# Retention heads one after the other, and the layer norms' work dealt out anew between DVE, ACT and POOL

## The chip, the cores and the metric

The kernel runs on the 8 cores of one Trainium2 chip, each core with its own sequence of 2048 tokens and a full copy of the weights; no core talks to another. Each core has TensorE (PE), VectorE (DVE), ScalarE (ACT), GpSimd (POOL) and a queue for transfers (SP). The metric is the device time of one launch in microseconds, that of the slowest core.

## What is computed

Two layers on x of shape (8, 2048, 1024), each an attention part and a feed-forward part with a plain layer norm (no scale or bias) behind each residual sum:

```python
# layer 0, attention part: an inner network of 2 blocks (i = 0, 1)
ln_x = layer_norm(x, ln1_g[i], ln1_b[i])
q, k, v, xo = split(ln_x @ proj_w[i] + proj_b[i], 4)      # 16 heads of 64
scores = einsum('bhld,bhmd->bhlm', q, k) * D               # D[n, m] = gamma_h**(n-m), 0 where m > n
ret = einsum('bhlm,bhmd->bhld', scores, v) * silu(xo)      # no softmax
x = x + ret @ reto_w[i] + reto_b[i]
h = layer_norm(x, ln2_g[i], ln2_b[i])
x = x + gelu(h @ ffn1_w[i] + ffn1_b[i]) @ ffn2_w[i] + ffn2_b[i]
# then layer_norm(x, lnf_g, lnf_b)
# layer 0, feed-forward: top-2 of 8 experts + shared expert
# layer 1: softmax attention over 1024 columns; block-diagonal rails, gelu, w_cproj
# x = _layernorm(x + part(x)) behind each of the four parts
```

## The kernel before

Activations lie feature-major: SX holds x in fp32 as 8 column tiles (ft) of 128 features by 2048 tokens, and the tokens are worked on in NB = 4 blocks (nb) of 512. A1, A2, A3 and PP hold bf16 operands, WR a ring of weights, pb0 to pb5 are PSUM banks of 128 x 512 fp32. The program is one list of instructions per engine, written in the order of the source; each engine runs its own list strictly in order. Every instruction of DVE, ACT and POOL waits for its own engine's previous one and for the tokens given (a token is a semaphore and a count). `bank_done` notes when a buffer is free, `bank_guard` returns that as a wait. `b.block()` makes all engines meet. Weights are issued on POOL's queue, so they stand behind POOL's compute instructions; masks, parking and the output are issued on SP's.

*Layer norm, `emit_ln`,* runs nine times. Five are affine (ln1 and ln2 of both blocks, lnf: scale and bias, result in bf16 in A1), four are plain (result in fp32 in SX, and a bf16 copy in A1). For each nb: eight casts to bf16 (L404 on ACT for ft 0, 3, 6, L407 on DVE for 1, 4, 7 and on POOL for 2, 5), eight squares on ACT (L420, two buffers), sixteen matmuls against a column of 1/1024 for mean and mean square (L425, L414, L431); then a chain on one row: ACT square L437, DVE L443 and L447, ACT logarithm and exponential L450 and L453, two broadcasting matmuls L460 and L464, two ACT copies of -mean and 1/std into SBUF (L469, L472). `emit_apply` adds and multiplies each of the eight tiles with these (L368, L371; even ft on DVE, odd on POOL) and is written one block late: the apply of block nb-1 stands in the source behind the copies of block nb, and the last two follow each other at the end. In affine norms ACT then scales each tile (L379). In plain norms the bf16 copy of a tile (L375) is made by the engine that did *not* apply it, so DVE and POOL wait for each other in each list.

*Retention, in `emit_l0_attn`,* runs for 2 blocks x 8 pairs of heads. Behind the four projections and 16 transposes of v comes, for each of 4 query blocks nb, a loop over key chunks mc = 0 to 4nb+3 of 128 keys. Per chunk and head h there is a score matmul (L954: 64 rows of q and k, head 0 on rows 0 to 63, head 1 on rows 64 to 127, into its own bank), an eviction to bf16 in MB (L973 on ACT for chunks below the diagonal, L980 on DVE with a mask for the four on it) and an accumulation (L933: all 128 rows, 64 columns, head 0 into partitions 0 to 63 of the result bank, head 1 into 64 to 127), two chunks behind its score. Both heads of a chunk are written next to each other; two chunks' slots form the ring. Then ACT copies the result out (L991) and DVE multiplies it with the gate (L996). Over nb that makes 8, 16, 24 and 32 (head, chunk) items.

*Layer-1 attention* begins by parking SX in DRAM (behind all of the norm before it) and by two small matmuls (L582) that spread the bias of v over PF (L587), the buffer in which the norm kept its -mean and 1/std.

## Time and profile before

| | us |
|---|---|
| median of the two runs | 10336.73 |
| lowest, highest run | 10178.47, 10494.99 |
| the profiled execution, its own time | 10140.04 |
| its span on the slowest core (core 4) | 10138.5 |
| spans of the other cores | 10075.2 to 10116.0 |
| stretch 150 to 1312 us, projections and retention of block 0 | 1162.00, PE busy 898.46, clock 0.64 |
| stretch 1312.00 to 1413.20, one affine norm | 101.20, PE 35.48, ACT 65.75, DVE 48.44, POOL 48.22 |
| stretch 4411.70 to 4559.60, one plain norm | 147.90, PE 35.77, ACT 40.64, DVE 41.27, POOL 55.62 |

How to read the rows further on. Times are microseconds from the start of the span. A timeline row gives start, duration (of all the instructions merged in it), engine, source line, operation, output <- input, shapes and count, and in brackets the idle time of the engine before it and what ended it. Matmuls are pipelined: their durations include filling the array, so the distance between starts says more than the duration. The clock is the share of TensorE's full speed that was granted; 0.50 is 1.2 GHz and 1.00 is 2.4 GHz. PEld are weight loads.

### The profile page before, as it was taken

The page shows a single profiled execution, that of the slowest core. Times are in us where ns is not written, and L with a number is a line of the kernel's source. Part 1 is how long each engine was busy: PE and PEld are TensorE (multiplying, and loading weights), DVE is VectorE, ACT ScalarE, POOL GpSimd, SP SyncE. Part 2 cuts the span into 40 slices and gives each one's busy share as a digit, 9 for nine tenths or more (in the row PEclk, how much of TensorE's full clock was granted, in tenths as well). Part 3 has the DMA queues.
Part 4 walks back from the last instruction along what each step waited for, and adds up shares of the span by engine and source line. Part 5 has one row for each costly group of instructions (what it writes and reads, how often), then busy time and mean ns, then how long its engine had stood idle before and what let it go on. Part 6 is the DMA issues. An engine that isn't in the chain of part 4 may idle for free. (4 is left out here: it accounts for less than half of the span.)

```text
span 10138.5 us, 89181 instructions; the slowest of 8 cores (10075.2 to 10138.5 us)
## 1 busy us (share of the span) xinstructions
PE 6911.8 (68%) x25254; PEld 2542.5 (25%) x25254; DVE 2044.2 (20%) x3440; ACT 2270.5 (22%) x3847; POOL 1086.0 (11%) x1144
## 2 busy tenths in 40 slices
PE   3777757767777577625778998874666347777774
PEld 1222212322222122202233443331222112222221
DVE  2222221122222301131111111211111212221222
ACT  3333230023333210232121222121111231112112
POOL 2000020010000200140011122121000210000002
PEclk7666667776666788857889999986777557787876
DMA  2000001101001011101111111201111111111110
GB/s 84 17 17 17 15 13 21 22 12 23 17 17 19 11 23 21 17 34 17 25 27 37 38 26 30 46 9 48 21 25 17 40 24 21 19 21 19 19 19 33
DMA packets 91864, 249.38 MB, mean 25 GB/s; under 512 B 13120, under 2 KB 15840, under 8 KB 87520
## 3 DMA queue, kind: packets, MB, share of 16 engines
q0 software_dynamic: 82688, 190.00, 11.2%
q1 hardware_dynamic: 8720, 53.68, 1.4%
q8 instruction: 239, 3.92, 0.2%
q14 instruction: 217, 1.78, 0.1%
HBM read 407.91 MB, written 25.72 MB: 43 GB/s over the span
## 5 line engine op out<-in xcount | busy, mean ns | idle before, releaser
L549 PE MATMUL pb<-A,WR 128*128 128x512 bf16 x5120 | 1419.2, 435 | 724.5 <-DMA WR<-ffn 207.1
L549 PEld LDWEIGHTS pb<-A,WR 128*128 128x128 bf16 x5120 | 547.0, 108 | 1595.3 <-issue 1245.2
L1570 PE MATMUL pb<-A,PP 128*128 128x512 bf16 x2688 | 669.7, 416 | 204.4 <-DMA PP<-wcT 148.0
L954 PE MATMUL pb<-PP 64*128 64x512 bf16 x1280 | 618.1, 596 | 88.8 <-ACT MB L973 42.9
L1069 PE MATMUL pb<-A,WR 128*128 128x512 bf16 x2048 | 533.0, 429 | 200.9 <-DMA WR<-ffn 200.9
L1578 DVE TENSOR_TENSOR SX<-SX,pb 128x512 f32<-128x512 f32 x512 | 352.2, 688 | 1470.5 <-PE pb L1570 1470.5
L1439 PE MATMUL pb<-A,WR 128*128 128x512 bf16 x2048 | 495.3, 408 | 170.1 <-DMA WR<-fc 170.1
L1530 ACT ACTIVATE A<-pb 128x512 bf16<-128x512 f32 x512 | 305.8, 597 | 1322.5 <-PE pb L1522 1247.6
L933 PE MATMUL pb<-MB,PP 128*64 128x512 bf16 x1280 | 473.3, 628 | 69.1 <-DVE MB L980 69.1
L425 PE MATMUL pb<-A,OM 128*1 128x512 bf16 x288 | 163.7, 588 | 518.3 <-ACT A L404 372.4
L980 DVE TENSOR_TENSOR MB<-pb,PF 128x512 bf16<-128x512 f32 x512 | 354.0, 691 | 710.2 <-PE pb L933 566.7
L973 ACT ACTIVATE MB<-pb 128x512 bf16<-128x512 f32 x768 | 458.6, 597 | 137.2 <-ACT MB L973 66.2
L1358 PE MATMUL pb<-A 128*128 128x512 bf16 x2048 | 455.3, 381 | 4.2 <-DMA A<-fc 4.2
L1380 PE MATMUL pb<-A 128*128 128x512 bf16 x2048 | 452.5, 379 | 0.0
L1035 ACT ACTIVATE A<-pb,CB 128x512 bf16<-128x512 f32 x256 | 175.9, 687 | 1152.0 <-PE pb L549 1122.4
L1570 PEld LDWEIGHTS pb<-A,PP 128*128 128x128 bf16 x2688 | 280.1, 105 | 594.0 <-issue 333.8
L1570 PE MATMUL pb<-A,WR 128*128 128x512 bf16 x1408 | 353.3, 418 | 109.0 <-DMA WR<-wcT 62.7
L1401 POOL TENSOR_TENSOR A<-A,PP 128x512 bf16<-128x512 bf16 x256 | 295.4, 1154 | 841.5 <-DVE A L1398 841.5
L1069 PEld LDWEIGHTS pb<-A,WR 128*128 128x128 bf16 x2048 | 218.2, 108 | 515.6 <-issue 354.4
L1368 ACT ACTIVATE A<-pb 128x512 bf16<-128x512 f32 x256 | 152.9, 597 | 868.1 <-PE pb L1358 866.7
L1522 PE MATMUL pb<-A 128*128 128x512 bf16 x512 | 261.5, 526 | 123.2 <-ACT A L1530 93.2
L1088 DVE TENSOR_TENSOR SX<-SX,pb 128x512 f32<-128x512 f32 x192 | 132.0, 688 | 1014.5 <-PE pb L1069 1014.5
(163 smaller groups left out, 6046.1 us busy)
## 6 DMA issues: line engine op xcount, KB each, us to landing
WR<-ffn POOLq DMA_DIRECT2D x128, 256.0 KB, 4.1
A<-fc POOLq DMA_DIRECT2D x8, 4096.0 KB, 22.5
PP<-wcT POOLq DMA_DIRECT2D x42, 512.0 KB, 5.2
WR<-w POOLq DMA_DIRECT2D x36, 512.0 KB, 5.2
A<-xpark SPq DMA_DIRECT2D x4, 4096.0 KB
WR<-fc POOLq DMA_DIRECT2D x32, 512.0 KB, 5.7
WR<-wcT POOLq DMA_DIRECT2D x22, 512.0 KB, 5.3
SX<-xin SPq DMA_DIRECT2D x1, 8192.0 KB
```

Source lines behind the costliest of these rows:

```text
L549: st=(kt == 0), sp=(kt == Kt - 1): e.matmul(bank[:, 0:512], sl[:, kt * 128:kt * 128 + 128], rhs, start=st, stop=sp),
L933: rbank=rbank: e.matmul(rbank[64 * h:64 * h + 64, 0:512], P1[:, mc * 128 + 64 * h: mc * 128 + 64 * h + 64], sT[2 * (mc % 2) + h], start=(m ...
L954: sb=sb: e.matmul(sb[:, 0:512], P3[64 * h:64 * h + 64, mc * 128:mc * 128 + 128], P2[64 * h:64 * h + 64, nb * 512:nb * 512 + 512], start=Tr ...
L973: e.activation(st, sb[:, 0:512], AF.Copy),
L980: off=off: e.tensor_mul(st, sb[:, 0:512], self.PF[:, off * 512:off * 512 + 512]),
L1069: e.matmul(bank[:, 0:512], sl[:, c * 128:c * 128 + 128], self.A2[:, c * T + nb * 512: c * T + nb * 512 + 512], start=st, stop=sp),
L1358: e.matmul(bank[:, 0:512], self.A3[:, (i * FT + kt) * 128: (i * FT + kt) * 128 + 128], self.A1[:, kt * T + nb * 512: kt * T + nb * 512 + 512],
L1380: e.matmul(bank[:, 0:512], self.A3[:, ((i + 8) * FT + kt) * 128: ((i + 8) * FT + kt) * 128 + 128], self.A1[:, kt * T + nb * 512: kt * T + ...
L1439: e.matmul(bank[:, 0:512], sl[:, it * 128:it * 128 + 128], self.A2[:, it * 2048 + nb * 512: it * 2048 + nb * 512 + 512], start=st, stop=sp ...
L1530: e.activation(self.A2[:, ci * 2048 + nb * 512: ci * 2048 + nb * 512 + 512], bk[:, 0:512], AF.Gelu),
L1570: e.matmul(bank[:, 0:512], sl[:, ci * 128:ci * 128 + 128], self.A2[:, ci * 2048 + nb * 512: ci * 2048 + nb * 512 + 512], start=st, stop=sp ...
L1578: e.tensor_add(self.SX[:, dt * T + nb * 512:dt * T + nb * 512 + 512], self.SX[:, dt * T + nb * 512:dt * T + nb * 512 + 512], bank[:, 0:512 ...
```

## The change

Four edits.

1. `emit_apply`: DVE applies six tiles and POOL two (ft 2 and 6). In plain norms the bf16 copies of tiles 2 and 6 are made by POOL, of 4 and 7 by DVE, of 0, 1, 3 and 5 by ACT. The casts in front of the statistics alternate between ACT (even ft) and DVE (odd); POOL has none.
2. The copies of -mean and 1/std go from ACT (L469, L472) to DVE.
3. The layer-1 attention's bias matmuls also wait for the end of the norm.
4. Retention: the loop runs over single items, all chunks of head 0 and then all of head 1. The ring has four single slots, and an accumulation stands four items behind its score.

```diff
@@ -362,7 +362,7 @@
         def emit_apply(nb, at, mtile, rtile):
             for ft in range(FT):
                 s = slice(ft * T + nb * 512, ft * T + nb * 512 + 512)
-                eng = ("vector", "gpsimd")[ft % 2]
+                eng = "gpsimd" if ft in (2, 6) else "vector"
                 sem = self.esem(eng)
                 tgt = self.SX if kind == "plain" else dst
                 b.emit(eng, lambda e, s=s, tgt=tgt, mtile=mtile: e.tensor_add(
@@ -371,9 +371,16 @@
                 b.emit(eng, lambda e, s=s, tgt=tgt, rtile=rtile: e.tensor_mul(
                     tgt[:, s], tgt[:, s], rtile), inc=((sem, 1),))
                 if kind == "plain":
-                    eng2 = ("gpsimd", "vector")[ft % 2]
-                    b.emit(eng2, lambda e, s=s: e.tensor_copy(
-                        self.A1[:, s], self.SX[:, s]), wait=(sem.tok(),))
+                    if ft in (2, 6):
+                        b.emit("gpsimd", lambda e, s=s: e.tensor_copy(
+                            self.A1[:, s], self.SX[:, s]))
+                    elif ft in (4, 7):
+                        b.emit("vector", lambda e, s=s: e.tensor_copy(
+                            self.A1[:, s], self.SX[:, s]))
+                    else:
+                        b.emit("scalar", lambda e, s=s: e.activation(
+                            self.A1[:, s], self.SX[:, s], AF.Copy),
+                            wait=(sem.tok(),))
                 if kind == "affine":
                     et = sem.tok()
                     b.emit("scalar", lambda e, s=s, ft=ft: e.activation(
@@ -398,7 +405,7 @@
             sqtok = [None] * FT
             for ft in range(FT):
                 s = slice(ft * T + nb * 512, ft * T + nb * 512 + 512)
-                ceng = ("scalar", "vector", "gpsimd")[ft % 3]
+                ceng = ("scalar", "vector")[ft % 2]
                 csem = self.esem(ceng)
                 if ceng == "scalar":
                     b.emit("scalar", lambda e, s=s: e.activation(
@@ -466,13 +473,13 @@
                 wait=rt, inc=((self.s_pe, 1),))
             self.bank_done(None, self.s_pe.tok(), ("SRr", par))
             bt = self.s_pe.tok()
-            b.emit("scalar", lambda e, pmean=pmean, mtile=mtile: e.activation(
-                mtile, pmean[:, 0:512], AF.Copy),
+            b.emit("vector", lambda e, pmean=pmean, mtile=mtile: e.tensor_copy(
+                mtile, pmean[:, 0:512]),
                 wait=(bt,) + self.bank_guard(None, ("PTm", par)))
-            b.emit("scalar", lambda e, psq=psq, rtile=rtile: e.activation(
-                rtile, psq[:, 0:512], AF.Copy),
+            b.emit("vector", lambda e, psq=psq, rtile=rtile: e.tensor_copy(
+                rtile, psq[:, 0:512]),
                 wait=self.bank_guard(None, ("PTr", par)))
-            at = self.s_act.tok()
+            at = self.s_dve.tok()
             self.bank_done(pmean, at)
             self.bank_done(psq, at)
             self.warm(wb, (at,))
@@ -583,7 +590,8 @@
                 bk[:, 0:512], self.O1[:],
                 self.MB[0:1, h * 512:h * 512 + 512],
                 start=True, stop=True),
-                wait=(dt0,) + self.bank_guard(bk), inc=((self.s_pe, 1),))
+                wait=(dt0,) + self.bank_guard(bk)
+                + getattr(self, "ln_done", ()), inc=((self.s_pe, 1),))
             b.emit("scalar", lambda e, h=half, bk=bk: e.activation(
                 self.PF[:, h * 512:h * 512 + 512], bk[:, 0:512], AF.Copy),
                 wait=(self.s_pe.tok(),), inc=((self.s_act, 1),))
@@ -922,70 +930,62 @@ (retention, the inner loops)
                 for nb in range(NB):
                     rbank = self.pb[4 + nb % 2]
-                    M = 4 * nb + 4
...
-                    def emit_mm2(mc, rbank=rbank, nb=nb, M=M):
-                        for h in range(2):
-                            b.emit("tensor", lambda e, h=h, mc=mc,
-                                   rbank=rbank: e.matmul(
-                                rbank[64 * h:64 * h + 64, 0:512],
-                                P1[:, mc * 128 + 64 * h:
-                                   mc * 128 + 64 * h + 64],
-                                sT[2 * (mc % 2) + h],
-                                start=(mc == 0), stop=(mc == M - 1),
-                                skip_group_check=True),
-                                wait=(evtok[mc][h],)
...
-                    for mc in range(M):
-                        for h in range(2):
-                            sb = self.pb[2 * (mc % 2) + h]
...
-                        mmt = self.s_pe.tok()
-                        if mc >= 2:
-                            emit_mm2(mc - 2)
-                        off = mc - 4 * nb
-                        stg = self.bank_guard(None, ("sTp", mc % 2))
-                        for h in range(2):
...
-                    for mc in range(max(0, M - 2), M):
-                        emit_mm2(mc)
+                LK = 4
...
+                    items = [(h, mc) for h in range(2)
+                             for mc in range(4 * nb + 4)]
+                    n_it = len(items)
+                    evtok = [None] * n_it
+
+                    def emit_mm2(i, rbank=rbank, items=items, nb=nb):
+                        h, mc = items[i]
+                        fs = (mc == 0)
+                        b.emit("tensor", lambda e, h=h, mc=mc, fs=fs, i=i:
+                               e.matmul(
+                            rbank[64 * h:64 * h + 64, 0:512],
+                            P1[:, mc * 128 + 64 * h:mc * 128 + 64 * h + 64],
+                            sT[i % LK], start=fs, stop=(mc == 4 * nb + 3)),
+                            wait=(evtok[i],)
...
+                    for i, (h, mc) in enumerate(items):
+                        sb = self.pb[i % LK]
...
+                        b.emit("tensor", lambda e, h=h, mc=mc, nb=nb, sb=sb:
+                               e.matmul(
+                            sb[:, 0:512],
+                            P3[64 * h:64 * h + 64, mc * 128:mc * 128 + 128],
+                            P2[64 * h:64 * h + 64, nb * 512:nb * 512 + 512],
+                            start=True, stop=True),
+                            wait=w0 + self.bank_guard(sb),
+                            inc=((self.s_pe, 1),))
                         mmt = self.s_pe.tok()
+                        if i >= LK:
+                            emit_mm2(i - LK)
+                        st = sT[i % LK]
+                        stg = self.bank_guard(st, ("sTm", i % LK))
...
+                        if off < 0:
+                            b.emit("scalar", lambda e, sb=sb, st=st:
+                                   e.activation(st, sb[:, 0:512], AF.Copy),
+                                   wait=(mmt,) + stg)
...
+                        else:
+                            b.emit("vector", lambda e, sb=sb, st=st, off=off:
+                                   e.tensor_mul(
+                                st, sb[:, 0:512],
+                                self.PF[:, off * 512:off * 512 + 512]),
+                                wait=(mmt, mskf) + stg)
...
+                    for i in range(max(0, n_it - LK), n_it):
+                        emit_mm2(i)
```

## Rows read from the trace of the kernel before

**Rows 1.** The page, part 1: busy us, share of span, instructions of each engine.

```profile
PE 6911.8 (68%) x25254; PEld 2542.5 (25%) x25254; DVE 2044.2 (20%) x3440; ACT 2270.5 (22%) x3847; POOL 1086.0 (11%) x1144
```

**Rows 2.** Window: length, busy PE PEld DVE ACT POOL, granted clock, DMA share, GB/s.

```profile
219.06:293.40 74.34, 64.06 (x160) 13.46 (x160) 23.76 (x36) 31.05 (x52) 1.09 (x3) 0.50 0.05 8
```

**Rows 3.** Timeline, PE, one pair's retention: start, us, engine, line, out<-in, count.

```profile
228.01 1.04 PE L954 MATMUL pb<-PP 64*128 64x512 bf16 x4
...
249.38 0.64 PE L933 MATMUL pb<-MB,PP 128*64 128x512 bf16 x2
249.96 0.60 PE L954 MATMUL pb<-PP 64*128 64x512 bf16 x1
250.42 0.58 PE L954 MATMUL pb<-PP 64*128 64x512 bf16 x1
250.93 0.64 PE L933 MATMUL pb<-MB,PP 128*64 128x512 bf16 x2
```

**Rows 4.** Timeline, ACT and DVE in retention: the two kinds of score eviction.

```profile
220.91 0.69 DVE L980 TENSOR_TENSOR MB<-pb,PF 128x512 bf16<-128x512 f32 x1 [0.24 <-DVE MB L980]
...
250.48 1.34 ACT L973 ACTIVATE MB<-pb 128x512 bf16<-128x512 f32 x2 [0.20 <-ACT MB L973]
...
292.34 0.60 ACT L991 ACTIVATE PT<-pb 128x512 bf16<-128x512 f32 x1 [8.21 <-PE pb L933]
```

**Rows 5.** Timeline, ACT, first affine norm: one whole turn of its loop.

```profile
111.25 0.59 ACT L437 ACTIVATE PF<-pb 1x512 f32<-1x512 f32 x1 [0.84 <-PE pb L431]
...
116.50 0.60 ACT L469 ACTIVATE PF<-pb 128x512 f32<-128x512 f32 x1 [1.64 <-PE pb L464]
...
118.11 7.54 ACT L379 ACTIVATE A<-A,CB 128x512 bf16<-128x512 bf16 x8
...
135.97 0.59 ACT L437 ACTIVATE PF<-pb 1x512 f32<-1x512 f32 x1 [1.05 <-PE pb L431]
```

**Rows 6.** Timeline, DVE, in that turn: alone, then beside POOL.

```profile
116.98 0.69 DVE L368 TENSOR_TENSOR A<-SX,PF 128x512 bf16<-128x512 f32 x1 [0.17 <-DVE A L371]
...
118.64 1.50 DVE L368 TENSOR_TENSOR A<-SX,PF 128x512 bf16<-128x512 f32 x1 [0.17 <-DVE A L371]
...
121.81 4.08 DVE L407 CAST A<-SX 128x512 bf16<-128x512 f32 x3
```

**Rows 7.** Timeline, end of the second affine norm and the stage behind it.

```profile
1394.49 0.60 ACT L469 ACTIVATE PF<-pb 128x512 f32<-128x512 f32 x1 [1.67 <-PE pb L464]
...
1409.46 2.21 POOL L96 DMA_DIRECT2D WR<-ffn  x4 [0.63 <-POOL A L371]
1409.47 3.70 ACT L379 ACTIVATE A<-A,CB 128x512 bf16<-128x512 bf16 x4 [1.46 <-DVE A L371]
...
1418.69 6.57 PE L549 MATMUL pb<-A,WR 128*128 128x512 bf16 x21 [22.40 <-DMA WR<-ffn]
```

**Rows 8.** Timeline, DVE, last plain norm: one turn of its loop and its end.

```profile
10033.55 0.69 DVE L443 TENSOR_TENSOR pb<-pb,PF 1x512 f32<-1x512 f32 x1 [8.40 <-ACT PF L437]
...
10046.28 0.43 DVE L375 CAST A<-SX 128x512 bf16<-128x512 f32 x1 [3.72 <-POOL SX L371]
...
10058.42 1.93 DVE L407 CAST A<-SX 128x512 bf16<-128x512 f32 x3
10068.32 0.69 DVE L443 TENSOR_TENSOR pb<-pb,PF 1x512 f32<-1x512 f32 x1 [7.97 <-ACT PF L437]
...
10116.19 0.43 DVE L375 CAST A<-SX 128x512 bf16<-128x512 f32 x1 [3.72 <-POOL SX L371]
```

**Rows 9.** Timeline, what starts behind two of the plain norms.

```profile
6935.31 0.58 POOL L96 DMA_DIRECT2D MB<-b3row  x1 [0.57 <-POOL SX L371]
6957.73 2.68 POOL L96 DMA_DIRECT2D WR<-w  x5 [21.84 <-ACTq L119]
...
8145.77 0.58 POOL L96 DMA_DIRECT2D PP<-makerT  x1 [0.58 <-POOL SX L371]
...
8154.66 0.33 PE L1480 MATMUL pb<-A,PP 16*16 16x64 bf16 x2 [50.93 <-PEq L119]
```

More of the change, by code:

```diff
@@ L924, in emit_l0_attn @@
                 sT = [self.MB[:, i * 512:(i + 1) * 512] for i in range(4)]
+                LK = 4
                 for nb in range(NB):
                     rbank = self.pb[4 + nb % 2]
-                    M = 4 * nb + 4
-                    evtok = [[None, None] for _ in range(M)]
-                    def emit_mm2(mc, rbank=rbank, nb=nb, M=M):
-                        for h in range(2):
-                            b.emit("tensor", lambda e, h=h, mc=mc,
-                                   rbank=rbank: e.matmul(
-                                rbank[64 * h:64 * h + 64, 0:512],
-                                P1[:, mc * 128 + 64 * h:
-                                   mc * 128 + 64 * h + 64],
-                                sT[2 * (mc % 2) + h],
-                                start=(mc == 0), stop=(mc == M - 1),
-                                skip_group_check=True),
-                                wait=(evtok[mc][h],)
-                                + (self.bank_guard(rbank)
-                                   if mc == 0 else ()),
-                                inc=((self.s_pe, 1),))
-                        self.bank_done(None, self.s_pe.tok(),
-                                       ("sTp", mc % 2))
@@ L947, in emit_l0_attn @@
-                    for mc in range(M):
-                        for h in range(2):
-                            sb = self.pb[2 * (mc % 2) + h]
-                            w0 = ()
-                            if nb == 0 and mc == 0 and h == 0:
-                                w0 = qk_attn + (vtm_done,)
-                            b.emit("tensor", lambda e, h=h, mc=mc, nb=nb,
-                                   sb=sb: e.matmul(
-                                sb[:, 0:512],
-                                P3[64 * h:64 * h + 64,
-                                   mc * 128:mc * 128 + 128],
-                                P2[64 * h:64 * h + 64,
-                                   nb * 512:nb * 512 + 512],
-                                start=True, stop=True),
-                                wait=w0 + self.bank_guard(sb),
-                                inc=((self.s_pe, 1),))
+                    items = [(h, mc) for h in range(2)
+                             for mc in range(4 * nb + 4)]
@@ new lines, in emit_l0_attn @@
+                    n_it = len(items)
[9 more added lines that the diff above has]
+                            wait=(evtok[i],)
+                            + (self.bank_guard(rbank)
+                               if (fs and h == 0) else ()),
+                            inc=((self.s_pe, 1),))
+                        self.bank_done(None, self.s_pe.tok(), ("sTm", i % LK))
@@ new lines, in emit_l0_attn @@
+                    for i, (h, mc) in enumerate(items):
+                        sb = self.pb[i % LK]
+                        w0 = (qk_attn + (vtm_done,)) \
+                            if (nb == 0 and i == 0) else ()
+                        b.emit("tensor", lambda e, h=h, mc=mc, nb=nb, sb=sb:
[5 more added lines that the diff above has]
+                            wait=w0 + self.bank_guard(sb),
+                            inc=((self.s_pe, 1),))
```

22 lines of the change are left out of this document (4 added, 18 removed).

## The prediction

> **What bounds the kernel now.** I read the list of cores first (all eight end close together, so one core can stand for all), then the page, then windows, then the timeline of the stages that the diff touches. TensorE (PE) is busy 68% of the span, ACT 22%, DVE 20% [rows 1], so outside the norms every stage is paced by PE or by the weights it waits for; the diff leaves those stages alone. It touches three places.
>
> *Retention* (16 head pairs, each over 74.3 us) runs with PE busy 64.06 of 74.34 us and the granted clock at 0.50, the lower level of 1.2 GHz, throughout [rows 2]. The reader is to see that "busy" hides a concurrency: four L954 matmuls of about 0.60 each take 1.04 together, so the two heads of a pair (rows 0-63 and 64-127) run side by side, and the next two start 1.04 - 0.60 = 0.44 later. The two L933 matmuls (columns 0-63 and 64-127) take 0.64 together in the same way [rows 3]. A turn of one key chunk, two heads, lasts 250.93 - 249.38 = 1.55 us [rows 3], which is two ACT evictions (1.34 and a gap of 0.20) [rows 4]: the evicting engine is the bound, at 0.77 an item, or 0.69 + 0.24 = 0.93 where DVE masks [rows 4].
>
> *Affine norms* (five) go round an ACT chain: 24.7 us from one L437 to the next, of which eight L379 take 7.54 [rows 5]. *Plain norms* (four) go round a lockstep of DVE and POOL: DVE stands 3.72 us before each L375 cast, waiting for POOL's multiply [rows 8].
>
> **Retention, after.** Heads run one after the other, so no two neighbouring matmuls can run side by side: consecutive L954s share the same 64 rows, L933s the same 64 columns. In the steady part each item is one score matmul and one accumulation, alternating. The trace shows both gaps between starts: L954 to L933, 250.93 - 250.42 = 0.51; L933 to L954, 249.96 - 249.38 = 0.58 [rows 3]. Together 1.09 us per item, more than 0.77 and 0.93: PE becomes the bound. Block nb has n = 8(nb+1) items: four scores to start (4 x 0.44), n - 4 items at 1.09, four accumulations to end (the first 0.14 earlier than an alternation would put it, then 3 x 0.44), and a switch (0.58). That is 1.09n - 0.84 (4 x 0.44 - 4.36 - 0.14 + 1.32 + 0.58 = -0.84). For n = 16, 24, 32 it gives 16.6 + 25.3 + 34.0 = 75.9 us. Before, the same three blocks last from 228.01 [rows 3] to 292.34 [rows 4], 64.3. The first block (n = 8, masked only) stays with DVE at 0.93 an item and costs nothing. So +11.6 per pair, x16 = **+186 us**. The deeper ring (four single slots) gives evictions slack, which no longer matters once PE binds. The bounds: matmuls of one kind with no switching cost would make 0.88 per item, then the evictions bind and the change is about 0; full durations end to end, 0.60 + 0.64 = 1.24 [rows 3], would make 72 items x 0.15 = 10.8 more per pair, +173 on top, +359. I take 1.09, since these very transitions are in the rows. The Trainium skill, page TensorEngine Tiling, section Key Properties, says that a change of tiling mode drains the engine; taken strictly that is the 1.24 of the upper bound, and the sum would be 359 instead of 186.
>
> **Affine norms, after.** A turn is counted from L437. The broadcast copies come at +5.25 (116.50 - 111.25) [rows 5], now on DVE. The trace has no such copy; it lies between DVE's cast of 0.43 [rows 8] and its PSUM operation of 0.69 [rows 4]. I take 0.69, it reads the same fp32 PSUM bank. Two end at +6.8, when ACT's two did. But DVE ran the apply of the block before *ahead* of that point (L368 at 116.98 is its third column tile) [rows 6]; now it stands behind the copies in DVE's queue and has six tiles instead of four. One tile (add and multiply) takes 118.64 - 116.98 = 1.66 us alone and 121.81 - 118.64 = 3.17 beside a working POOL [rows 6]. POOL's two tiles of the new block start at the same moment and take two of DVE's with them: 2 x 3.17 + 4 x 1.66 = 13.0, so DVE ends at +19.9. Behind each tile stands ACT's L379; the last ends one L379 later (7.54 / 8 = 0.94), +20.9, and only then does ACT start the next block's casts and squares. Those took 135.97 - (118.11 + 7.54) = 10.3 [rows 5]; with a fourth ACT cast, partly in its waits for PE, 10.8. Turn: 31.7 against 24.7, +7.0. Two such turns in five norms: **+70**. If POOL did not slow DVE, the turn would be 3.0 shorter: +40.
>
> The end of the norm: before, 1413.17 - 1394.49 = 18.7 us from the last copies to the last L379 [rows 7]. After: 1.7 + 13.0 + 10.0 (six tiles alone) + 1.0 = 25.7. PE, though, did not start at 1413.17 but at 1418.69, 9.2 us after POOL had issued the weights [rows 7]. POOL ends its share by 1394.49 + 1.7 + 2 x 3.2 = 1402.6, so weights are there by 1411.8, and PE starts when the norm ends, 1420.2: +1.5 instead of +7.0. The early DMA gives back most. Four norms that stand before weights: +6; the fifth, before a parked-input transfer that waits for the whole norm: +7. Affine norms in all **+83**.
>
> **Plain norms, after.** No cast crosses between DVE and POOL any more, so the 3.72 us waits go. Turn from one L443: copies at +4.6 (5.25 less 0.69), done at +6.1; six tiles, two contended (13.0), two casts of 0.43 and gaps (1.2), and 0.8 for POOL's casts in the same ports: 15.0, +21.1; then as before 10068.32 - 10058.42 = 9.9 from the next casts [rows 8], and 0.5 for ACT's extra cast: 31.6 against 34.8. Two turns in four norms: -26. The end: before 10116.62 - 10068.32 = 48.3 [rows 8]; after 6.1 + 15.0 + 11.2 = 32.3: -16, x4 = -64. ACT's four casts per block lie beside DVE's tiles. Where POOL issues a load behind the norm, as for the rail weights (issued 8145.77, PE 8154.66), it now issues it while DVE still works: -8 [rows 9]. In all **-98**.
>
> **The added guard** in the layer-1 attention costs nothing: the next weights are issued at 6957.73, after the parking transfer of about 22 us that itself waits for the norm [rows 9]; two small matmuls and two evictions lie under it. Without that cover it would cost them, some 2.5 us.
>
> **Sum.** 186 + 83 - 98 = +171. The profiled execution took 10140.04 us: 10311. The two runs shown have the median 10336.73 (10178.47 and 10494.99), 1.9% above the profiled one; on their scale 10508. I give the middle, **10410**, since the rows can't say which the next runs resemble. Relative to like: +1.7%. About 2% is what a measurement of this kernel can tell from no change.
>
> **The rivals.**
> *Full drain* (slower): item 1.24, retention +359, net +344, +3.4%, 10484 to 10680. For it: each matmul lasts 0.60 or more. Against: starts 0.51 and 0.58 apart. It decides from about 1.12 per item upwards (net +203, 2%). 0.15.
> *Free switch* (no change): single matmuls follow at 0.44 whatever the kind; evictions bind, retention 0, net -15. For it: the measured gaps are always those of pairs. 0.15.
> *Quiet ports* (no change): POOL's fewer operations rarely meet DVE's, turns 3.0 shorter, ends 3.0 shorter: 9 norms x 9 = -80, net about +90. Against: both start on the same copy. 0.12.
> *Higher clock* (faster): with PE issuing without a pause in retention, the clock rises, PE stops binding, and with head runs alternating, ACT's and DVE's evictions overlap. Evictions alone, 0.77 x 8nb + 7.4, are 13.6 + 19.7 + 25.9 = 59.2; about three items overlapped at each of three turns (2.2 us each) save 6.6 per block, and some 1.5 per block is lost at its ends: 44, so -20 per pair, -320, and net -335: -3.3%, 9805 to 10000. Against: 0.50 over a stretch with PE busy 86% [rows 2]. The Trainium skill, TensorE: Matmul & The Clock Gate, Part 1, says that the throttled clock is the default and activity releases it; by that rule this rival would come true. 0.08.
>
> **How the numbers follow.** My forecast has 0.50, with its own range of 10200 to 10590 (net +60 to +250 on the two scales). Slower by over 2%: the full drain and a third of my own, 0.33. Faster by over 2%: the higher clock and a little, 0.09. Within: 0.58. The range drops the higher clock and the upper end of the full drain: free switch on the lower scale is 10125, forecast and half of the drain's reach 10600. I take 10150 to 10600.
>
> **What would show it.** Right: retention's L954 and L933 starts alternate at 0.51 and 0.58, the stretch of one pair about 86 us with PE busy nearly all of it, clock 0.50; affine norm turns near 31.7 with DVE the releaser of L379; plain turns near 31.6, no 3.72 waits. Wrong: a clock above 0.50 in retention; matmuls of different heads overlapping; L379 runs of eight without gaps.

## The result, and the profile after

| | before | after |
|---|---|---|
| median, us | 10419.21 (10 runs, 10091.11 to 10494.99) | 10364.17 (11 runs, 10302.50 to 10665.32) |
| the profiled execution | 10140.04 | 10290.51 |
| span, median of its eight cores | 10096.1 | 10271.8 |
| like with like | 1 | 1.0193, 95% interval 1.0135 to 1.0251 |

In many executions of either kernel the cores of one die or both run at a lower granted clock and take up to 6% longer, so the medians stand the wrong way round, the last row leaves those executions out, and "undisturbed cores" here are the four of a die at the highest clock seen for its kernel. Like with like the changed kernel is 1.9% slower. The interval lies clear of no change, but it contains 2%, so on which side of 2% the change lies stays undecided. Undisturbed cores of the kernel before take 10059 to 10110 us (clock 0.76 to 0.77), those of the changed one 10248 to 10308 (the same clock).

The page of the changed kernel, part 1 and the groups of retention (part 5: line, engine, operation, count, busy us, mean ns, idle time before and what ended it). L945 is the accumulation, L960 the score, L975 and L981 the two evictions:

```profile
PE 7160.2 (70%) x25254; PEld 2603.1 (25%) x25254; DVE 2231.1 (22%) x3660; ACT 2293.2 (22%) x3875; POOL 854.2 (8%) x896
...
L945 PE MATMUL pb<-MB,PP 128*64 128x512 bf16 x1280 | 745.6, 618 | 19.8 <-DVE MB L981 19.7
L960 PE MATMUL pb<-PP 64*128 64x512 bf16 x1280 | 699.1, 580 | 29.1 <-ACT MB L975 12.7
...
L975 ACT ACTIVATE MB<-pb 128x512 bf16<-128x512 f32 x768 | 459.0, 598 | 446.2 <-PE pb L945 387.1
L981 DVE TENSOR_TENSOR MB<-pb,PF 128x512 bf16<-128x512 f32 x512 | 354.2, 692 | 882.4 <-PE pb L945 834.6
```

PE's busy time rose from 6911.8 [rows 1] to 7160.2 for the same number of matmuls, and in retention PE hardly waits any longer, 19.8 and 29.1 us in 1280 matmuls each. The two groups of the kernel before (page, part 5) had 88.8 and 69.1:

```profile
L954 PE MATMUL pb<-PP 64*128 64x512 bf16 x1280 | 618.1, 596 | 88.8 <-ACT MB L973 42.9
...
L933 PE MATMUL pb<-MB,PP 128*64 128x512 bf16 x1280 | 473.3, 628 | 69.1 <-DVE MB L980 69.1
```

Both evicting engines wait for PE instead, 446 and 882 us (137 and 710 before). That is the change of bound that the prediction named. Two pairs' stretches (windows; PE, PEld, DVE, ACT, POOL busy, granted clock), answering to [rows 2]:

```profile
235.42:320.80 85.38, 81.18 (x160) 17.99 (x160) 23.83 (x36) 31.08 (x52) 1.18 (x3) 0.55 0.04 7
799.10:876.26 77.16, 72.26 (x160) 17.40 (x160) 23.84 (x36) 31.08 (x52) 1.18 (x3) 0.65 0.04 8
```

and the steady part (timeline, PE), answering to [rows 3]:

```profile
252.51 0.63 PE L945 MATMUL pb<-MB,PP 128*64 128x512 bf16 x1
253.08 0.60 PE L960 MATMUL pb<-PP 64*128 64x512 bf16 x1
253.62 0.63 PE L945 MATMUL pb<-MB,PP 128*64 128x512 bf16 x1
```

One item takes 253.62 - 252.51 = 1.11 us, 0.57 from accumulation to score and 0.54 on to the next accumulation (over many items 1.10). The 16 stretches of this core sum to 1368.6 us against 1190.5 before, so retention costs **+178**.

One turn of the first affine norm (timeline; L444 and L386 answer to L437 and L379 of [rows 5], the DVE rows to [rows 6], L476 is a copy):

```profile
87.36 0.59 ACT L444 ACTIVATE PF<-pb 1x512 f32<-1x512 f32 x1 [0.83 <-PE pb L438]
97.44 0.81 ACT L386 ACTIVATE A<-A,CB 128x512 bf16<-128x512 bf16 x1 [6.59 <-DVE A L371]
...
120.06 0.59 ACT L444 ACTIVATE PF<-pb 1x512 f32<-1x512 f32 x1 [1.05 <-PE pb L438]
...
92.33 0.69 DVE L476 COPY PF<-pb 128x512 f32<-128x512 f32 x1 [2.81 <-PE pb L471]
...
93.99 1.78 DVE L368 TENSOR_TENSOR A<-SX,PF 128x512 bf16<-128x512 f32 x1 [0.17 <-DVE PF L479]
95.88 1.47 DVE L371 TENSOR_TENSOR A<-A,PF 128x512 bf16<-128x512 bf16 x1
...
106.94 0.69 DVE L371 TENSOR_TENSOR A<-A,PF 128x512 bf16<-128x512 bf16 x1
```

The turn lasts 120.06 - 87.36 = 32.7 us (24.7 before), and ACT, which went round without a pause, now waits for DVE in front of L386. From the start of a norm to the next matmul of other work the five affine norms take 125.8, 127.6, 127.4, 127.8 and 127.2 us, against 111.1, 107.6, 108.2, 106.5 and 102.4: **+100**. The last plain norm (timeline, ACT and DVE), answering to [rows 8]:

```profile
10201.18 0.59 ACT L444 ACTIVATE PF<-pb 1x512 f32<-1x512 f32 x1 [1.05 <-PE pb L438]
...
10233.39 0.59 ACT L444 ACTIVATE PF<-pb 1x512 f32<-1x512 f32 x1 [1.04 <-PE pb L438]
...
10264.36 0.63 ACT L381 ACTIVATE A<-SX 128x512 bf16<-128x512 f32 x1 [3.22 <-DVE SX L371]
...
10266.03 0.43 DVE L378 CAST A<-SX 128x512 bf16<-128x512 f32 x1
```

Its turn is 32.2 us, the whole norm 127.2 instead of 147.9, and the waits of 3.72 are gone. Four norms give back 83, and PE starts 3 us earlier behind the first and 8.5 earlier behind the one ahead of the rail weights: **-95**. The sum, 178 + 100 - 95 = +183, stands beside +176 between the medians of the cores' spans.

### The profile page after: what moved, and what is told of

Read it like the earlier page. It is cut to its first block and busy times, and to the rows that moved or that the text cites. A ratio compares the mean times of both kernels' runs of the same rounds, so it can differ in the third digit from the quotient of the medians.

```text
span 10288.6 us, 89699 instructions; the slowest of 8 cores (10256.0 to 10288.6 us)
## 1 busy us (share of the span) xinstructions
PE 7160.2 (70%) x25254; PEld 2603.1 (25%) x25254; DVE 2231.1 (22%) x3660; ACT 2293.2 (22%) x3875; POOL 854.2 (8%) x896
## 5 line engine op out<-in xcount | busy, mean ns | idle before, releaser
L556 PE MATMUL pb<-A,WR 128*128 128x512 bf16 x5120 | 1384.5, 427 | 742.6 <-DMA WR<-ffn 165.8
L945 PE MATMUL pb<-MB,PP 128*64 128x512 bf16 x1280 | 745.6, 618 | 19.8 <-DVE MB L981 19.7
L960 PE MATMUL pb<-PP 64*128 64x512 bf16 x1280 | 699.1, 580 | 29.1 <-ACT MB L975 12.7
L1069 PE MATMUL pb<-A,WR 128*128 128x512 bf16 x2048 | 516.8, 419 | 201.0 <-DMA WR<-ffn 201.0
L1439 PE MATMUL pb<-A,WR 128*128 128x512 bf16 x2048 | 497.1, 409 | 168.2 <-DMA WR<-fc 168.2
L975 ACT ACTIVATE MB<-pb 128x512 bf16<-128x512 f32 x768 | 459.0, 598 | 446.2 <-PE pb L945 387.1
L981 DVE TENSOR_TENSOR MB<-pb,PF 128x512 bf16<-128x512 f32 x512 | 354.2, 692 | 882.4 <-PE pb L945 834.6
L1570 PE MATMUL pb<-A,WR 128*128 128x512 bf16 x1408 | 352.9, 418 | 107.8 <-DMA WR<-wcT 62.4
```

The source lines that it names most:

```text
L556: st=(kt == 0), sp=(kt == Kt - 1): e.matmul(bank[:, 0:512], sl[:, kt * 128:kt * 128 + 128], rhs, start=st, stop=sp),
L945: e.matmul(rbank[64 * h:64 * h + 64, 0:512], P1[:, mc * 128 + 64 * h:mc * 128 + 64 * h + 64], sT[i % LK], start=fs, stop=(mc == 4 * nb + 3)),
L960: e.matmul(sb[:, 0:512], P3[64 * h:64 * h + 64, mc * 128:mc * 128 + 128], P2[64 * h:64 * h + 64, nb * 512:nb * 512 + 512], start=True, sto ...
L975: e.activation(st, sb[:, 0:512], AF.Copy),
L981: e.tensor_mul(st, sb[:, 0:512], self.PF[:, off * 512:off * 512 + 512]),
L1069: e.matmul(bank[:, 0:512], sl[:, c * 128:c * 128 + 128], self.A2[:, c * T + nb * 512: c * T + nb * 512 + 512], start=st, stop=sp),
```

## The experiments

**The norms alone, and retention alone.** The first kernel has edits 1 to 3 without 4, the second edit 4 alone.

```diff
 # norms alone: the retention loops are those of the kernel before
 # retention alone, against the changed kernel:
...
-                ceng = ("scalar", "vector")[ft % 2]
+                ceng = ("scalar", "vector", "gpsimd")[ft % 3]
...
 # and the other lines of edits 1 to 3 as in the kernel before
```

> The changed kernel with the retention loop of the kernel before. Theory A (the three terms of the prediction add up and do not touch each other): each retention stretch back to 74.3 us from 86, the five affine norms stay near 127 us and the four plain ones near 127, so the profiled time lies about 178 us under that of the changed kernel and within 15 us of the kernel before (+100 for the affine norms with what follows them, -95 for the plain ones); ratio to before 0.998 to 1.003. Rival B (norm changes cost more than their own stretches, through later weights or a lower clock behind them): ratio above 1.006 with the stretches as in theory A.

> The kernel before with the retention loop of the changed kernel. Theory A: 16 stretches of about 86 us instead of 74.3, all norms as before; ratio to before 1.016 to 1.020. Rival B (retention is slowed by something that the norm changes bring, such as the order in which DVE is handed work): stretches below 80 us and a ratio below 1.008.

The norms alone: undisturbed cores 10062 to 10097 us, which is the kernel before. Windows of a retention stretch, of an affine and of a plain norm:

```profile
232.19:306.98 74.79, 64.06 (x160) 13.46 (x160) 23.83 (x36) 31.05 (x52) 1.18 (x3) 0.50 0.05 8
1291.70:1418.40 126.70, 36.97 (x84) 7.88 (x84) 63.61 (x80) 64.35 (x93) 24.03 (x20) 0.50 0.05 9
4440.90:4568.60 127.70, 37.28 (x84) 7.85 (x84) 68.46 (x88) 48.42 (x77) 30.11 (x25) 0.50 0.01 1
```

Retention alone: 1.0182 of before (1.0138 to 1.0226), the same windows of a stretch and an affine norm:

```profile
218.65:304.49 85.84, 82.55 (x160) 18.05 (x160) 23.83 (x36) 31.07 (x52) 1.18 (x3) 0.52 0.04 7
1383.50:1485.20 101.70, 35.57 (x84) 7.59 (x84) 49.30 (x52) 66.59 (x97) 49.03 (x44) 0.52 0.02 3
```

The whole slowdown is retention's. The two halves add up without touching each other: affine norms lose what plain norms win, and neither moves the 74.8 or the 85.8 of a stretch.

**Order of the heads, or order on PE?** The changed kernel with the two heads alternating again from item to item, still one score and one accumulation in turn:

```diff
-                    items = [(h, mc) for h in range(2)
-                             for mc in range(4 * nb + 4)]
+                    items = [(h, mc) for mc in range(4 * nb + 4)
+                             for h in range(2)]
...
```

> The changed kernel with its items ordered chunk by chunk with the two heads next to each other, but still one score and then one accumulation at a time, with the ring of four single slots. Theory A (two matmuls run side by side only where they are neighbours in PE's list and of the same kind): nothing comes back, stretches 85 to 87 us, starts still about 0.54 and 0.56 apart. Rival C (it is enough that successive items use different heads, or the cost lies in the head order): stretches return to 74 to 77 us, the total about 170 us under the changed kernel.

All 16 stretches last 86.4 to 86.8 us; undisturbed cores take 10275 to 10313. Timeline, PE (L961 is the score):

```profile
251.47 0.63 PE L945 MATMUL pb<-MB,PP 128*64 128x512 bf16 x1
252.03 0.60 PE L961 MATMUL pb<-PP 64*128 64x512 bf16 x1
252.56 0.63 PE L945 MATMUL pb<-MB,PP 128*64 128x512 bf16 x1
```

Still 1.09 us an item. So it is not the run of one head that costs, as the prediction's text had it. It is the single score standing between two single accumulations: no two matmuls that could run side by side are neighbours in PE's list.

**What a change of kind costs.** Items in twos: two scores, then two accumulations, of the same head, so that nothing can run side by side but there are half as many changes.

```diff
-                    for i, (h, mc) in enumerate(items):
...
+                    for i0 in range(0, n_it, 2):
+                        mmts = []
+                        for i in (i0, i0 + 1):
...
+                            mmts.append(self.s_pe.tok())
+                        if i0 >= LK:
+                            emit_mm2(i0 - LK)
+                            emit_mm2(i0 + 1 - LK)
+                        for i in (i0, i0 + 1):
...
```

> The changed kernel with the heads still one after the other, but two scores and then two accumulations at a time, so that two of each kind are neighbours on the same rows or columns: half as many switches between the kinds and no side-by-side running. Theory A (an item costs one start distance within a kind, 0.44, or one across kinds, 0.54 and 0.56): four matmuls in 0.43 + 0.54 + 0.43 + 0.56 = 1.96 us for two items, 0.98 an item instead of 1.10; 72 items give 8.6 us less per stretch, so 77 to 79 us (the evictions on DVE, 0.93 to 1.0, leave little room), about 125 us off the total. Rival D (the switch itself costs nothing, the 1.10 is set by two weight loads and two waits per item): stretches stay at 85 to 87 us. Rival E (any two neighbours of one kind run side by side): stretches near 74 us.

Timeline, PE (L963 is the score):

```profile
252.09 1.03 PE L963 MATMUL pb<-PP 64*128 64x512 bf16 x2
253.05 1.06 PE L945 MATMUL pb<-MB,PP 128*64 128x512 bf16 x2
254.04 1.03 PE L963 MATMUL pb<-PP 64*128 64x512 bf16 x2
```

Two items take 1.95 us, 0.98 each against 1.10, with two changes in place of four. So a change costs about (2.20 - 1.95) / 2 = 0.12 us, and what remains is 4 x 0.43: four matmuls at their bare distance at 1.2 GHz. A stretch is 81.3 to 82.4 us; undisturbed cores take 10193 to 10215, some 75 less than the changed kernel. That is less than expected, because the expectation let all 72 items gain. In the second stretch of each kernel the first query block, eight masked items, takes 9.6 us in both, since DVE's evictions are the bound there. The later blocks take 16.0, 23.5 and 31.7 us instead of 16.6, 24.9 and 34.3: the 1.95 for two items holds in their steady part, masked or not, while a block's start and its end each take 0.1 to 0.3 us longer.

**The place of the two copies.** The changed kernel with the copies of -mean and 1/std back on ACT, nothing else.

```diff
-            b.emit("vector", lambda e, pmean=pmean, mtile=mtile: e.tensor_copy(
-                mtile, pmean[:, 0:512]),
+            b.emit("scalar", lambda e, pmean=pmean, mtile=mtile: e.activation(
+                mtile, pmean[:, 0:512], AF.Copy),
...
```

> The changed kernel with only the two copies of -mean and 1/std back on ACT; the rest (six tiles on DVE, two on POOL, retention by heads) stays. Theory A (what slows the affine norms is the place of the copies: the apply of the block before now stands behind them in DVE's queue, and they wait for PE): DVE starts its six tiles right behind its two one-row operations, 4.4 us earlier than after (89.6 instead of 94.0 in the first norm), so the turn of an affine norm falls from 32.7 to about 28, each norm, affine or plain, from 127.4 to about 113 us (three applies of four start earlier), nine norms give back about 125 us, and an undisturbed die ends near 10140 instead of 10254 to 10300. Theory B (what slows them is DVE's work, six tiles and two more operations): only the 1.6 us of the two copies come back per turn, the turn is about 31, a norm about 121, nine norms 58 us, an undisturbed die near 10210. Theory C (POOL and DVE slowing each other sets it): no change, 127, 10270. The retention stretches stay at 86.

Timeline, ACT and DVE of the first norm:

```profile
89.89 0.59 ACT L444 ACTIVATE PF<-pb 1x512 f32<-1x512 f32 x1 [0.83 <-PE pb L438]
...
117.76 0.59 ACT L444 ACTIVATE PF<-pb 1x512 f32<-1x512 f32 x1 [1.05 <-PE pb L438]
...
91.37 0.68 DVE L454 TENSOR_SCALAR MB<-pb 1x512 bf16<-1x512 f32 x1
92.23 0.69 DVE L368 TENSOR_TENSOR A<-SX,PF 128x512 bf16<-128x512 f32 x1 [0.17 <-DVE MB L454]
```

DVE starts the tiles 0.17 us behind its one-row work, where the changed kernel had them wait for the copies (93.99 against 88.85 + 0.68). The turn is 27.9 us, an affine norm 113.0, a plain one 113.5; undisturbed cores take 10133 to 10180, about 125 less. Theory A holds: some 14 of the 20 us that an affine norm lost (to the next matmul of other work: 107.4 in the kernel before, 127.5 in the changed one, 113.6 here) come from edit 2 alone, and plain norms lost them too.

**POOL's two tiles.** The changed kernel with all eight tiles of an affine apply on DVE.

```diff
-                eng = "gpsimd" if ft in (2, 6) else "vector"
+                eng = "gpsimd" if ft in (2, 6) and kind == "plain" \
+                    else "vector"
```

> The changed kernel with all eight tiles of an affine norm's apply on DVE, none on POOL; plain norms and the rest as in the changed kernel. Theory A (the price in the prediction: a DVE tile takes 1.66 alone and 3.2 beside a working POOL, so POOL's two tiles cost DVE about as much as they spare it): eight tiles take 13.3 against the 13.6 measured in a turn, the two turns per norm change by 0.3 at most, at the end sixteen tiles take 26.6 against 23.3, an affine norm 129 to 131 us instead of 127.5. Theory B (POOL spares DVE its two tiles, and the slow tiles beside it had another cause, the first tiles behind the copies): the first tiles stay slow, 3.2, the turn grows by 3.3 and the end by 6.6, an affine norm takes about 140 us.

One execution of it was run. Timeline, DVE and ACT of the first norm (L369, L372, L445 are L368, L371, L444 of the changed kernel):

```profile
95.54 0.69 DVE L369 TENSOR_TENSOR A<-SX,PF 128x512 bf16<-128x512 f32 x1 [0.17 <-DVE PF L480]
96.33 0.69 DVE L372 TENSOR_TENSOR A<-A,PF 128x512 bf16<-128x512 bf16 x1
...
108.37 0.69 DVE L372 TENSOR_TENSOR A<-A,PF 128x512 bf16<-128x512 bf16 x1
...
88.91 0.59 ACT L445 ACTIVATE PF<-pb 1x512 f32<-1x512 f32 x1 [0.82 <-PE pb L439]
121.21 0.59 ACT L445 ACTIVATE PF<-pb 1x512 f32<-1x512 f32 x1 [1.04 <-PE pb L439]
```

The first tiles behind the copies take 0.69 an operation, not 1.78 and 1.47: it was POOL beside them. Eight tiles take 13.5 us where six with POOL's help took 13.6, the turn is 32.3 against 32.7, a later norm 129.8 against 127.4. POOL's two tiles spare DVE nothing in a turn; only at the end of a norm, where the last two applies follow each other, do they spare 3.3 us. In the changed kernel both engines start one operation in 1.6 us while both work, in turns: DVE at 95.88 and 97.52, POOL at 95.37 and 97.00. The Trainium skill, SBUF — State Buffer, section Who interferes with whom, says that a DVE instruction with two SBUF inputs contends with a GpSimd instruction that reads SBUF, over a pair of ports that is locked exclusively. The trace agrees with the contention and the turns; but 0.69 and POOL's 1.16 to 1.26 alone would add up to 1.9, more than the 1.6 seen, so the two do not shut each other out for their whole durations.

**Why the plain norms were long.** The kernel before with one edit: each engine casts the tiles it has itself applied, four and four as before (the guard of edit 3 goes with it).

```diff
-                    eng2 = ("gpsimd", "vector")[ft % 2]
-                    b.emit(eng2, lambda e, s=s: e.tensor_copy(
-                        self.A1[:, s], self.SX[:, s]), wait=(sem.tok(),))
+                    b.emit(eng, lambda e, s=s: e.tensor_copy(
+                        self.A1[:, s], self.SX[:, s]))
```

> The kernel before with one thing altered: in plain norms each engine makes the bf16 copy of the tiles it has itself applied, so nothing crosses between DVE and POOL; four tiles each as before, statistics and copies as before, retention as before. (The guard on the layer-1 bias matmuls goes with it, since the norm's last copies then end later than those matmuls could start.) Theory A (the lockstep of crossing casts is what made a plain norm 147.9 us long): DVE's four tiles with casts take about 15 us and POOL's about 16.5 instead of 23.2 for the two together, four times in a norm: a plain norm takes 118 to 122 us, four of them save about 110 to 120 with the gaps behind them, an undisturbed die ends near 9970. Theory B (it is the dealing of six tiles to two that made the changed kernel's plain norms shorter; POOL's four tiles and casts, slowed by DVE beside them, take about as long as the lockstep did): 140 us or more, an undisturbed die near 10060. Affine norms stay at 102 and the retention stretches at 74.

Timeline, DVE, the last plain norm: the apply of one block, first and last row.

```profile
9869.49 0.69 DVE L368 TENSOR_TENSOR SX<-SX,PF 128x512 f32<-128x512 f32 x1 [0.17 <-DVE MB L446]
...
9880.42 1.30 DVE L374 CAST A<-SX 128x512 bf16<-128x512 f32 x1
```

One block's apply takes DVE 12.2 us instead of 23.2 (10058.42 less the 10035.26 at which it began there), a plain norm 108 us (148 before, 118 to 122 expected): DVE's first two tiles, at 0.69 an operation, are done before POOL starts its own. It is shorter than in any kernel above; undisturbed cores take 9899 to 9941, 1.6% less than before. The second kernel puts the changed kernel's dealing (six to two, casts on three engines) into the plain norms of the kernel before:

```diff
-                eng = ("vector", "gpsimd")[ft % 2]
+                if kind == "plain":
+                    eng = "gpsimd" if ft in (2, 6) else "vector"
+                else:
+                    eng = ("vector", "gpsimd")[ft % 2]
 # and the casts of edit 1
```

> The kernel before with only the plain norm's apply as in the changed kernel (six tiles on DVE, two on POOL, casts on the three engines); the copies of -mean and 1/std stay on ACT, the casts in front of the statistics stay on three engines, affine norms and retention as before. Theory A (the parts of the change are separate, and a plain norm gains more where DVE's queue has no copies in front of the tiles): a plain norm takes 113 to 118 us (127.2 in the changed kernel, 147.9 before), four save about 120 to 140, and with the gaps behind them 150 to 170; an undisturbed die ends near 9930, 0.984 of before. Theory B (the plain norm needs the whole new dealing, its statistics casts too): about 127, 0.99. Affine norms stay at 102, retention stretches at 74.

A plain norm takes 111 us, undisturbed cores 9900 to 9932. So the crossing casts were the cause of the long plain norms; the new dealing adds nothing. The changed kernel, at 127.2, gives 16 of these 37 us back, 14 of them by edit 2 (113.5 with the copies on ACT).

**Retention the other way.** Both heads of a chunk next to each other as before, the four masked chunks spread among the others, unmasked evictions shared between ACT and DVE, accumulations three chunks behind; norms as in the kernel just shown.

```diff
...
+                    for j in range(4):
+                        order += offd[j * nb:(j + 1) * nb]
+                        order.append(4 * nb + j)
...
+                                eng = "scalar" if h == 0 or k % (nb + 1) == (0 if nb == 1 else 1) \
+                                    else "vector"
...
```

> As the kernel with only the plain apply altered, plus another order in retention: both heads of a chunk stay next to each other, the four masked chunks stand spread among the others, the ACT work is shared with DVE (head 1 of most unmasked chunks), four chunks of bf16 slots, and the accumulation three chunks behind. Theory A (before, one evicting engine at a time sets the pace, 0.77 or 0.93 an item, while the other stands idle; PE itself needs 1.09 for both heads of a chunk, 0.51 and 0.58 between kinds): with both engines evicting at once a chunk costs about 1.1 to 1.2 us instead of 1.55 and 1.86, a pair's stretch 48 to 55 us instead of 74, sixteen save 310 to 400, and an undisturbed die ends near 9600, 0.95 of before. Theory B (a matmul on one half of the array costs 1.10 per item with its switch, whatever stands beside it, as in the changed kernel): the stretches are 80 to 87 us, and the total is at 1.00 of before or above. Theory C (a clock lowered further in the dense stages gives a part back): stretches as in A, but the dense stages longer and the total above 0.965.

Timeline, PE (L972 score, L950 accumulation, two heads in each row):

```profile
249.81 0.71 PE L972 MATMUL pb<-PP 64*128 64x512 bf16 x2 [0.61 <-DVE A L1006]
250.45 0.64 PE L950 MATMUL pb<-A,PP 128*64 128x512 bf16 x2
251.02 0.60 PE L972 MATMUL pb<-PP 64*128 64x512 bf16 x2
...
252.21 0.71 PE L972 MATMUL pb<-PP 64*128 64x512 bf16 x2
...
253.74 0.74 PE L972 MATMUL pb<-PP 64*128 64x512 bf16 x2 [0.26 <-DVE A L1006]
```

Two heads take 1.2 us together where a chunk is unmasked, 1.53 where both are masked and DVE must do two evictions in a row. A stretch is 63.1 to 64.8, not 48 to 55; undisturbed cores take 9739 to 9769, 0.968 of before. The mechanism of theory A held (theory B, 80 or more, did not); the size was off. The masked chunks kept their waits, and in the first stretch two chunks across the end of a block take 4.6 to 5.0 us where 2.4 is the rule.

**One item of each head, of different chunks.** So in a turn one item may be masked (DVE) and the other not (ACT), and the turns of all four query blocks form one list. In the norms each engine casts the plain tiles that it has itself applied.

```diff
...
+                    for k, pr in enumerate(zip(dg + of, of + dg)):
+                        turns.append((nb, k, M, pr))
...
+                for g in range(len(turns) + LG):
...
```

> Retention once more, from what the runs so far showed (a change of kind on PE costs about 0.1 us, two heads next to each other run side by side, each evicting engine alone needs 0.80 to 0.93 an item). A turn now has one item of each head, but of different chunks, so that in every turn from the second query block on DVE evicts one item (masked, or a plain copy where neither is masked) and ACT one; the turns of all four query blocks are one list, with accumulations three turns behind, so that no block ends with PE waiting. Norms as in the kernel before, with each engine casting its own plain tiles. Theory A (PE's two switches and the pair's own length bind, 1.10 per turn, evictions 0.93 at most beside it): 36 turns at 1.10 and four masked ones at 1.86 at the start make 47, some 3 for start and end, a stretch of 50 to 52 us (64 with whole chunks masked on DVE, 74 before), sixteen save 370 to 390 against before, with the 157 of the norms an undisturbed die ends near 9540, 0.945 of before. Theory B (the round trip score, eviction, next score on the same bank binds, 0.7 and 0.7 and 0.15 = 1.55 for two turns' banks each used every second turn, so never): as A. Theory C (what made the spread chunks cost 1.2 and 1.5 was not two evictions in a row on one engine): stretches stay near 60 to 64, an undisturbed die near 9740.

Windows of the first and third stretch, and in the second fence the timeline of PE (L976 score, L940 accumulation):

```profile
217.79:265.64 47.85, 40.96 (x160) 11.73 (x160) 32.14 (x48) 23.88 (x40) 1.18 (x3) 0.80 0.07 12
422.89:472.83 49.94, 41.92 (x160) 11.55 (x160) 32.14 (x48) 23.88 (x40) 1.18 (x3) 0.74 0.07 12
```

```profile
244.97 0.61 PE L976 MATMUL pb<-PP 64*128 64x512 bf16 x2
...
246.08 0.61 PE L976 MATMUL pb<-PP 64*128 64x512 bf16 x2
...
258.76 0.66 PE L976 MATMUL pb<-PP 64*128 64x512 bf16 x2
...
259.69 0.67 PE L976 MATMUL pb<-PP 64*128 64x512 bf16 x2
```

A turn of two items takes 246.08 - 244.97 = 1.11 us at the lower clock, half of what the changed kernel pays (1.10 for one). Stretches are 47.4 to 50.0 us (74 before, 86 after). Not all of that is the new order: the granted clock here is 0.74 and 0.80, where the kernel before had 0.50, and at 1.00 a turn takes 259.69 - 258.76 = 0.93 us. The 50 to 52 us of the expectation were worked out with 1.10 a turn, so by an estimate some 1 to 3 of the 24 to 27 us that a stretch gains come from the clock, the rest from the order. Undisturbed cores take 9493 to 9557 us against 10059 to 10100 of the kernel before beside it, whole executions at their best 9550.6 against 10099.6 and 10099.9: 0.945, between 0.940 and 0.950 by the extremes of the cores. This version beats both kernels.

## Why the prediction was right or wrong

**Retention, right.** The two gaps of [rows 3] were the right rows: 0.51 and 0.58 forecast, 0.54 and 0.57 measured, the stretch 85.9 forecast, 86.2 measured where the clock stays low. +178 instead of +186, because one of this core's sixteen stretches took 77 us (on other cores one to three). The full drain in the prediction's sense (1.24 an item) is refuted by every steady row. By the Trainium skill, TensorEngine Tiling (Array Packing), section Key Properties, a change of tiling mode drains the engine; it names no price. The trace does not agree with the reading that the prediction took strictly, whole durations end to end: a change costs 0.12 us. Whether a short emptying of the array lies behind these 0.12 us no run here shows. A free switch is refuted too. One reading was right only in its sum: the text put the loss down to heads running one after the other, and the run with alternating heads shows that the alternation of single scores and accumulations suffices.

**Affine norms, right mechanism, undersized: +83 against +100.** The turn is 32.7 to 33.1, not 31.7: tiles began at +6.6 and took 13.6 (forecast 6.8 and 13.0), the last L386 ended at +21.4 (20.9), and ACT took 11.3 from there (10.8). Two turns make +16.7 in the second norm instead of +14.0; the beginning of that norm, taken as unchanged, is 1.1 longer; and the end gave back less, +2.3 against +1.5. That is +20 where +15.5 stood. The last affine norm gave +24.8 against 21.

**Plain norms, right: -98 against -95.** Turn 32.2 (31.6 forecast; its terms add up to 31.5), the last part, from the last L450 (the L443 of before) at 10234.08, 32.4 (32.3 forecast, 48.3 before), the rail weights -8.5 (forecast -8). That POOL slows DVE was right as well, so the quiet ports did not come true.

**The guard, right:** from the start of the norm in front of it to the first matmul behind the parking it is 160.0 us instead of 181.3, and 20.8 of these 21.4 are the norm's gain, so nothing of a guard is seen.

**The higher clock, right to leave small, but not absent.** Windows of the changed kernel in one stretch, before, during and after the start of a query block:

```profile
246.00:257.00 11.00, 11.00 (x22) 2.22 (x20) 3.30 (x6) 4.54 (x8) 0.00 (x0) 0.50 0.01 1
...
262.00:265.10 3.10, 2.30 (x9) 0.58 (x7) 0.43 (x1) 2.29 (x5) 0.00 (x0) 1.00 0.00 0
265.60:272.00 6.40, 6.40 (x13) 1.36 (x12) 2.76 (x4) 2.39 (x4) 0.00 (x0) 0.50 0.00 0
```

PE had been busy without a pause at 0.50, the last 2.5 us of it with accumulations alone and then scores alone (from 259.12), when the clock went to 1.00 for some 3 us, in which the pace was ACT's 0.80 an item, and fell back to 0.50 while busy without a pause. This is the rival's mechanism in miniature; it is worth 9 us in a stretch that has much of it (77.16, where the clock stood at 1.00 over the last 24 us).

**The step that failed is the last, how a sum became a time.** The terms gave +171, or +1.7% like with like; measured were +176 between cores and +1.93%. On its own scale the sum gave 10311, and the profiled execution took 10290.51. But the text then set the two quoted runs of before (10178 and 10495, 317 us apart) beside its own sum as a second scale and took the middle, 10410. That number belongs to no execution: it is the sum plus 99 us that have nothing to do with the change, more than the error of any term (17 at most). Against the 10336.73 then shown it says +0.7%, no change, and so the forecast's first number denied its own working. The clock and span of every core were there for the profiled execution, and all eight ended close together; with the two other times 38 and 355 us above it, it should have been the only base.

The chances took the same fault in. "About 2% is what a measurement can tell" was too coarse: like with like the half width is 0.6%, so +1.7% was a slowdown that would be told from nothing. And two thirds of the own forecast went to "within 2%" although its sum stood close to that edge; the measured interval reaches over the edge as well, so no chance on either side of it is borne out. With the plain and retention terms resting on rows to within some 10 us, the working supported: slower, by some 1 to 2.5% (an estimate).

## What to carry to other kernels

Make the sum against one profiled execution whose cores end together, and keep it on that scale. Where two matmuls use different halves of the array, their worth lies in being neighbours in PE's list; to alternate single ones of two kinds costs the concurrency and a change each. And before work is dealt anew between engines, look at what crosses: one cast moved to the engine that already had the tile was worth about 165 us here (10083 and 9918 in the middle of the undisturbed cores), the whole new dealing nothing more, and two copies in front of work that was ready cost 125.

## What the runs showed of the hardware that was not expected

- A matmul of another kind behind a half-array matmul starts 0.54 to 0.57 us later at 1.2 GHz, one of the same kind 0.43 to 0.44; a change costs 0.12 us.
- Two half-array matmuls on different halves, four instructions a turn with two changes of kind, take 1.10 us together, as long as two instructions with two changes when each stands alone.
- A DVE operation on two SBUF operands takes 0.69 us alone and 1.5 to 1.8 beside POOL, POOL's own rises from 1.26 to 1.46. With POOL silent the same rows return to 0.69.
- In retention the granted clock stays at 0.50 over 11 us of a PE without a pause, yet stood at 0.74 and 0.80 in the stretches of the paired version, where PE is busy 84 to 86%. What decides this was not settled; one thing that any account must meet: the kernel with alternating heads never saw a shortened stretch, the changed one one to three in sixteen.
